# The last chunk's output stage laid out by two batches and 64 tokens, half of it run inside that chunk, and the second half of the preparation convolved by taps alone

## The reference

```python
x = x + _L0_cond_ref(x, ..., cond_2048, 16)          # attention, 16 heads
x = x + _L1_cond_ref(x, cond_2048, W_in, W_conv, ...)

def _L1_cond_ref(x, t_emb, W_in, W_conv, b_conv, ln_g, ln_b, W_xproj, W_dt, b_dt, A_log, D, W_out):
    xr, gate = jnp.split(x @ W_in.T, 2, axis=-1)     # 1024 channels each
    xr = xr + t_emb[:, None, :]
    xc = silu(causal_conv_of_4_taps(xr, W_conv) + b_conv)
    xn = layernorm(xc) * ln_g + ln_b
    Bm, Cm, dt = jnp.split(xn @ W_xproj.T, 3, axis=-1)   # 16 states each
    dt = jnp.tanh(dt @ W_dt.T + b_dt) * 0.01
    Ad = 1.0 + dt * A
    Bd = Bm * jnp.minimum(jnp.linalg.norm(xn, axis=-1, keepdims=True), 1.0)
    def step(h, inputs):                             # 1024 steps, one after the other
        ad, bd, xt, ct = inputs
        h = jnp.clip(h * ad[:, :, None] + bd[:, :, None] * xt[:, None, :], -10.0, 10.0)
        return (h, jnp.einsum('bd,bdh->bh', ct, h))
    _, ys = jax.lax.scan(step, h0, ...)
    y = ys + D * xn
    return y * jax.nn.silu(gate) @ W_out.T
```

## Time and profile before

| | us |
|---|---|
| median of three runs (6010.3 to 6031.31) | 6021.95 |
| profiled execution | 6045.26 |
| its span | 6043.3 |
| attention and the first half of the preparation | 0 to 3212.8 |
| second half of the preparation | 3212.8 to 3353.2 |
| recurrence, chunks 0 to 6 | 3353.2 to 5673.7 |
| recurrence, chunk 7 | 5673.7 to 5957.5 |
| tail | 5957.5 to 6043.3 |

### The profile page before, as it was taken

How to read it: one execution, slowest core, us unless ns; L and a number is a source line. 1 busy time by engine, 2 the same in 40 slices (tenths; PEclk the granted TensorE clock), 3 DMA queues, 4 the chain that set the end, 5 groups by cost and what they waited for, 6 DMA issues and landing times.

```text
span 6043.3 us, 74674 instructions
## 1 busy us (share of the span) xinstructions
PE 5770.7 (95%) x24986; PEld 2610.9 (43%) x24986; DVE 4388.4 (73%) x5652; ACT 2411.4 (40%) x4726; POOL 3185.9 (53%) x2561
## 2 busy tenths in 40 slices
PE   7999999999999999999989999999999999999999
PEld 3444444444444444444435434434344444434334
DVE  4656556565565656656534899999999999999994
ACT  2444444444444444444445333434243433434110
POOL 1777667776676767666664142434434242434313
PEclk7999999999999999999999999999999999999999
DMA  2332323323233232322322444444445344444543
GB/s 88 84 99 64 100 60 112 96 66 102 60 109 95 63 102 62 114 82 58 99 70 105 107 123 107 125 133 122 137 113 151 99 143 110 133 126 124 140 116 122
DMA packets 415984, 622.82 MB, mean 103 GB/s; under 512 B 59088, under 2 KB 192336, under 8 KB 415088
## 3 DMA queue, kind: packets, MB, share of 16 engines
q1 hardware_dynamic: 378736, 567.68, 33.2%
q10 hardware_dynamic: 36864, 50.38, 3.3%
HBM read 310.56 MB, written 205.57 MB: 85 GB/s over the span
## 4 chain that ended last, share of the span: by engine, by line
PE 70%; DVE 18%; issue 4%; ACT 2%; ACTq 2%; POOL 2%; DMA 1%; DVEq 1%; SPq 0%; POOLq 0%
DVE g L2223 9%; PE bank L820 8%; PE bank L850 8%; PE bank L808 6%; PE miscb L1979 5%; PE misc L837 5%; PE yps L1940 5%; DVE g L2229 5%; PE bank L779 3%; PE bank L761 3%; PE miscb L1871 3%; PE bank L789 3%; PE yps L1871 3%; PE xps L1926 2%; PE miscb L1950 2%
## 5 line engine op out<-in xcount | busy, mean ns | idle before, releaser
L1161 POOL TENSOR_TENSOR acc<-acc,prob 128x512 f32<-128x512 f32 x1536 | 1908.1, 1279 | 853.9 <-PE bank L850 571.7
L1090 DVE TENSOR_REDUCE mx<-bank 128x1 f32<-128x512 f32 x2048 | 1308.2, 686 | 542.7 <-PE bank L820 536.5
L2223 DVE SCALAR_TENSOR_TENSOR g<-xps,bd,g 128x1024 f32<-128x1024 f32 x1024 | 1313.1, 1282 | 118.9 <-PE xps L1926 89.6
L983 ACT ACTIVATE prob<-misc 128x512 f32<-128x512 f32 x1277 | 713.5, 598 | 760.7 <-PE misc L837 675.1
L820 PE MATMUL bank<-khat,qhat 96*128 96x512 f32 x2048 | 940.5, 520 | 20.5 <-DVE xt_s L1067 15.3
L2229 DVE TENSOR_SCALAR g<-g,lim 128x1024 f32<-128x1024 f32 x1024 | 832.1, 813 | 34.6
L837 PE MATMUL misc<-qhat,khat 98*128 98x512 f32 x1443 | 602.6, 460 | 18.2 <-ACT prob L983 12.4
L820 PEld LDWEIGHTS bank<-khat,qhat 96*128 96x128 f32 x2048 | 374.0, 192 | 548.7 <-issue 383.1
L1940 PE MATMUL yps<-g,cexp 128*32 128x512 f32 x4096 | 499.8, 606 | 0.0
L808 PE MATMUL bank<-xhT,wqk 128*128 128x512 f32 x1024 | 490.2, 605 | 2.6 <-ACT rsum L989 1.7
L850 PE MATMUL bank<-prob,V 128*32 128x512 f32 x3584 | 488.9, 615 | 0.2 <-ACT prob L983 0.2
(11 more groups left out here) (246 smaller groups left out, 7752.3 us busy)
## 6 DMA issues: line engine op xcount, KB each, us to landing
sx<-scratch_xhl SPq DMA_DIRECT2D x512, 128.0 KB, 5.3
scratch_dx<-dx SPq DMA_DIRECT2D x64, 512.0 KB, 2.8
scratch_xhl<-xhi SPq DMA_DIRECT2D x64, 512.0 KB, 4.0
scratch_xhl<-xn SPq DMA_DIRECT2D x64, 512.0 KB, 4.7
scratch_y<-ysb SPq DMA_DIRECT2D x512, 64.0 KB
early<-scratch_dx SPq DMA_DIRECT2D x59, 512.0 KB, 4.7
early<-scratch_y SPq DMA_DIRECT2D x59, 512.0 KB, 3.6
xt_n<-in_x SPq DMA_DIRECT2D x112, 256.0 KB, 3.0
```

Of the source, the lines that this page charges most:

```text
L983: act.activation(to, bank[m][:, 0:QC], ACT.Exp, scale=SCALE).then_inc(sem[f"act_m{m}"], 1)
L1090: dve.tensor_reduce(self.mx2[:, h * TT + qt, c:c + 1], bank[m][:, 0:QC], AX.X, ALU.max).then_inc(sem[f"dve_m{m}"], 1)
L1161: pool.tensor_tensor(self.acc[:, a, h, :], self.acc[:, a, h, :], self.prob[:, (n % 2) * GH + h, :], ALU.add).then_inc(sem["pool_acc"], 1)
L2223: dve.scalar_tensor_tensor(self.g[:, t % STATES, :], self.xps[t % 2][:, :], self.bd[:, i % 2, tl:tl + 1], self.g[:, (t - 1) % STATES, :], ...
```

## The change

The change has four parts.

- **Preparation.** `by_matmul` no longer names the channel tiles 1, 3, 5 and 7 of chunk 0's second half. They are convolved by taps.
- **Output stage of chunk 7.** A tile is now two batches and 64 tokens (`last_rows`): tiles 0 to 3 hold the first 64 tokens of all eight batches, tiles 4 to 7 the last 64. Tiles 0 to 3 run in room 1 inside chunk 7, due from 0.55 to 0.97 of it. Tiles 4 to 7 are the tail, in rooms 0 (4 and 7), 1 (5) and 2 (6). Each load and store of such a tile is two DMAs of 64 partitions instead of one of 128. The gates are loaded back between 0.02 and 0.5 of the chunk.
- **Planner's numbers.** `PE_LATE` goes from 0.3 to 0.2. In the preparation, fillers come only for gaps over 0.9 and in banks 3, 1 and 0. The ends of the lanes move a little.
- Chunk 6's output stage is due 0.1 of a chunk before the end of chunk 7, so that it doesn't meet the end.

```diff
-PE_LATE = 0.3
+PE_LATE = 0.2
-LAST_ROOMS = 3
+LAST_ROOMS = (4, 7), (0, 1, 2, 3, 5), (6,)
+def last_rows(b, TOK):
+    h, pair = divmod(b, 4)
+    return [(slice(64 * k, 64 * k + 64), 2 * pair + k, slice(h * TOK // 2, (h + 1) * TOK // 2)) for k in range(2)]
 def by_matmul(i, hb, ct):
-    return ct in ((2,5) if i == 1 else (1, 3, 5, 7) if (i, hb) == (0, 1) else ())
+    return ct in ((2,5) if i == 1 else ())
...
-    order.warm = (0.6, 0.15, 0.45, (3, 1, 0, 2))
+    order.warm = (0.9, 0.3, 0.45, (3, 1, 0))
...
+    order.warm = (0.6, 0.15, 0.45, (3, 1, 0, 2))
     order.lane(steps())
     for i in range(NCH):
         t = i * TOK
-        order.lane(expand(i, range(1, TOK // WIDE)), t - 4.0, t + 0.8 * TOK)
+        order.lane(expand(i, range(1, TOK // WIDE)), t - 4.0, t + 0.7 * TOK)
         if i + 1 < NCH:
-            order.lane(convolve(i + 1, SIDE), t + -8.0, t + 0.627 * TOK)
-            order.lane(rows(i + 1, SIDE), t + 0.143 * TOK, t + 0.937 * TOK)
+            order.lane(convolve(i + 1, SIDE), t + -8.0, t + 0.637 * TOK)
+            order.lane(rows(i + 1, SIDE), t + 0.144 * TOK, t + 0.937 * TOK)
         if i:
-            order.lane(finish(i - 1, SIDE, 0, range(B)), t + -8.0, t + TOK + (0.0 if i < NCH - 1 else -3.0))
+            order.lane(finish(i - 1, SIDE, 0, range(B)), t + -8.0, t + TOK + (0.0 if i < NCH - 1 else -0.1 * TOK))
...
         if i == NCH - 1:
-            order.lane(back(), t + 0.1 * TOK, t + 0.9 * TOK)
+            order.lane(back(), t + 0.02 * TOK, t + 0.5 * TOK)
+            order.lane(finish(i, SIDE, 1, range(4)), t + 0.55 * TOK, t + 0.97 * TOK)
     order.run(lambda: ("g", last - 1) in order.done)
     order.late = None
-    for room in range(LAST_ROOMS):
-        order.lane(finish(NCH - 1, ALL, room, range(room, B, LAST_ROOMS)), last - 1.0, last - 1.0)
+    for room, some in enumerate(LAST_ROOMS):
+        order.lane(finish(NCH - 1, ALL, room, [b for b in some if b >= 4]), last - 1.0, last - 1.0)
...
-                sp.dma_start(self.room[rm]["y"][:, :], d["y"][b, i * TOK:(i + 1) * TOK, :]).then_inc(sem[f"ld_y{rm}"], 16)
+                for rows, c, some in self.rows_of(i, b):
+                    sp.dma_start(self.room[rm]["y"][rows], d["y"][c, some, :]).then_inc(sem[f"ld_y{rm}"], 16)
```

63 lines of the change are left out of this document (39 added, 24 removed).

## The result

The changed kernel takes 5984.94 us (median of six runs, 5981.13 to 5998.19) and the kernel before 6021.61 us (six runs beside it, 6010.3 to 6031.31). The ratio is 0.9943, with an interval from 0.9928 to 0.9958: 36.7 us less, where 43 were forecast. The profiled execution took 5998.19 us with a span of 5996.4, 47 us less than the profiled one of before.

The account below looks back on a forecast made before the run. No engine was full in the preparation's second half; DVE bounds the recurrence and PE the tail. Tail 30, preparation 11, chunks between 9, less 7 in chunk 7, make 43 us: 6022 to 5979 us, with 5953 to 6004 holding 8 in 10.

Parts of the forecast that it names:

- The sum: Whole kernel: 30 + 11 + 9 - 7 = 43 us less, 6022 to 5979 us.
- The tail: After the last `g`: four of eight PE tiles go, 31.0 us less 1.0 us of small costs, 30 us gained.
- the preparation: Second half of the preparation: taps replace matmuls and `nrm` comes earlier, 11 us gained, bounds 4 and 17 us.
- the chunks between: Chunks 1 to 6: shorter waits for `x` through the limit of 0.2, 1.5 us a chunk, 9 us gained.
- chunk 7: Last chunk: four more `oo` on DVE cost 2.7 us and added waits for `x` 4.3 us, 7 us lost.
- three small things: Tail: second DMA of the first `y` tile 0.3 to 0.4 us, last tile's `om` wait 0.25, split last store 0.35.
- I am wrong if the tail isn't under 60 us: Sign for the tail: from the last `g` to the end 56 us was expected instead of 85.8.
- Rival 2: Chunk 7: PE's list stops for late `fs` or loads, two 2.1 us waits per tile, 17 us lost, 5995 us; chance 0.11.
- nrm comes at 3279 to 3280 instead of 3290.28: Preparation: after earlier transposes, store, statistics and root, `nrm` on ACT comes earlier, the basis of the 11 us gain.
- From there POOL is full for 40 us as before: Preparation, from `nrm` on: POOL works 40 us without a break and the end of the preparation is unchanged.
- rival 1: Preparation: twelve taps cost POOL's first half 9 us, the preparation gains only 2 us, 5988 us; chance 0.13.
- Rival 4: Seven chunks: PE's clock falls once more in each, DVE waits 4.9 us, 34 us lost, 6013 us; chance 0.07.

Follow-up runs that it names:

- a_fill: The changed kernel with more fillers in the tail (54 behind the last outputs instead of 39): 5979.72 us, tail 62.6 us.
- b_split: The kernel before, last chunk's output-stage loads and stores as two DMAs of 64 neighbouring partitions each: 6034.54 us, tail 90.3 us.
- b_even: The kernel before, last chunk's output-stage loads and stores as two DMAs, one of even and one of odd partitions: 6020.47 us, tail 88.4 us.
- a_first: The changed kernel with the last lanes due 3.5 steps later, so SP stores the last outputs before loading `D * xn`: 5983.63 us, tail 64.4 us.
- b_wolate: The kernel before with the load of `w_out` put off to the first chunk: 6018.27 us, preparation 134.8 us.
- a_matmul: The changed kernel with the preparation's four channel tiles convolved by matmul again: 5988.07 us, preparation 138.1 us.
- b_late2: The kernel before with `PE_LATE` at 0.2 instead of 0.3 and nothing else: 6019.73 us, chunks 0 to 6 2318.6 us.
- b_lanes: The kernel before with only the changed kernel's three due times of the loop's lanes: 6027.17 us, chunks 1 to 6 1982.8 us.
- a_loopfill: The changed kernel with more fillers on PE in the loop (idle gap 0.4 us instead of 0.6): 5987.03 us.
- a_one: The changed kernel with one DMA per load and store, two batches by 64 tokens in one pattern, instead of two: 6125.22 us.

## Why the prediction was right, point by point

**The sum.** -43 forecast, -36.7 by the medians and -40.0 by the stages that the change touches. The sign and the stages are those forecast; the terms are not. The tail gave 8.6 us less than forecast and the preparation 2.6 less; the chunks between gave 4.5 more and chunk 7 cost 3.7 less. That the sum comes within 3 us is in part luck.

**The tail, the mis-sized term.** "The tail gives 31.0 - 1.0 = 30 us": it gave 21.4. The four tiles did go at the price forecast. In a_fill, with its fillers, the tail behind the first `yt` takes 36.2 us, and the forecast's 56 us less the 19.9 up to it are 36.1. The mistake is in the "three small things" that come back. I priced two DMAs of 64 partitions by the time to issue the second, 0.3 to 0.4 us, and took their rate for granted. The traces show 5.9 us up to the first transpose; in the three other traces with the order of the changed kernel's tail it is 4.9 to 5.7, and their tails take 63.0 to 63.6 us. b_split has the part that the split alone costs, 2.6 us, and b_even shows that 2.2 of it are the rate of neighbouring partitions. The other 3.3 us are argued and not isolated by a run. The loads of `D * xn` stood 3.7 us ahead of the last `g` in the kernel before and now stand behind a store of chunk 7, 0.8 us ahead: 1.5 MB meet the last outputs on their way. a_first shows that this can't be had back by moving the store. That the two halves of a load now come from two batches is a rival that no run separates from it. Last, PE ran out of fillers over the longer wait, and its clock cost 2.3 us (a_fill). 5.9 + 2.3 = 8.2 of the 8.6 us that the term is short. "I am wrong if the tail isn't under 60 us": this step was wrong.

**Chunk 7.** +3.3 us, where 2.7 + 4.3 were forecast. Four `oo` more of 0.68 us are 2.7 us by their durations, and DVE's busy time rose by 2.1. The waits rose from 2.2 to 3.1 us, and not by 4. The denser end of the chunk costs almost nothing, since the order puts the tiles between the `x`. Rival 2 is refuted by the longest wait of 1.1 us.

**The preparation.** -8.4 us for -11, but by another way. The step "nrm comes at 3279 to 3280 instead of 3290.28" fell short. The stage begins 6.8 us earlier in the trace of the change, so it has to be read from the stage's start: forecast were 10 to 11 us less, and `nrm` starts 69.8 us after it where it started after 77.5, 7.7 less. It was lost at the taps. They were to end near 3260.5, 47.7 us after the start, and end after 53.9: DVE is busy with the last twenty-one for 27.3 us, within the 31 of the forecast, but it stops for 6.0 us among them, 3.4 of that for one scaling on ACT. `hi` and `sq` stand behind the last silu on ACT's list, and the first half's last `lo` ends after 61.6 us, with 57.8 forecast and 67.6 before. "From there POOL is full for 40 us as before" failed: it took 45.8 us, with stops of 3.99 and 0.89 us for ACT and 1.54 for a store, since ACT now has the attention's evictions among its copies. I moved `f_mm` of tiles 2 to 4 behind the projections on PE and didn't follow their evictions on ACT's list. These are -7.7 and +6.4 us; the other -7.1 came behind the last `lo`. What made up for the lost time stood in brackets as a bound: the load of `w_out`. That it came out near the forecast is luck. b_wolate gives 5.7 us by it alone, and of the 6 us that a_matmul loses, 5.3 lie between the last `lo` and the first `q`, behind that load. As to what taps and POOL cost each other: POOL's pairs of passes beside the taps took 2.94 to 3.41 us instead of 2.50, which makes 5.4 us over the first half and 1.8 in the kernel before. The twelve more taps cost POOL 3.6 us, 0.30 us each, between the 0.15 of the rows and the 0.75 that the rule of the Trainium skill (SBUF — State Buffer, Who interferes with whom) comes to if taken strictly. It cost the kernel nothing, since each group of slowed passes ends in a stop of POOL for ACT (5.41, 1.30 and 0.34 us); rival 1 priced the loss at 9 us and fell. DVE paid more: its eighteen taps beside POOL took 1.39 us on average, where one alone takes 0.78, and ACT's work stood behind them.

**The chunks between.** -13.5 us for chunks 0 to 6 where -9 was forecast, and the cause given was wrong. `PE_LATE` alone gives nothing (b_late2). The lanes' due times do it (b_lanes), +3.0 us in chunk 0 and 3.4 us off each of chunks 2 to 5. The forecast took the stretches at the lower clock as given and shortened the short waits; it gave 0.5 us to what had moved in such a stretch. The traces show the reverse: the time at the lower level falls from 13.7 to 6.8 us a chunk in chunks 2 to 5, and the 3.4 us go with it. Rival 4, that the clock falls once more in each chunk, didn't come; the opposite did. Its price of 4.9 us was a fair one: chunk 5 of a_loopfill, where it did fall, took 4.8 us more than its neighbour.

## What to carry to other kernels

Before a tile is laid differently over the partitions, read the rate of the DMAs that fill it in the last two columns of a window: a half-tile of 64 neighbouring partitions moved at 0.6 of the rate with the engines just as busy, and a pattern with an outer dimension of two ran at the share of two engines of sixteen. Where a stage ends in a short load that everything waits for, look at what else was sent for in the 20 us before; a 2 MB load there cost 6 us, and moving it is one line. When work leaves one engine's list, follow the results of that work on the next engine's list, since that is where part of the gain went here. And before a few microseconds in a loop are put down to an edit, compare the same chunk in traces of the same order, and the time that each spent at the lower clock: here that alone made 3.3 us of 331.

## What the runs showed that was not expected

- The rate by partitions: 383 GB/s for DMAs of 128 partitions, 234 and 237 for 64 neighbouring ones, 279 at a share of 0.84 for 64 alternate ones. Laying the changed kernel's two batches on even and odd partitions would join the two; it wasn't tried.
- One DMA over [2, 64] rows: share 0.13, 53 GB/s.
- An issue can cost far more than the 0.33 to 0.6 us that most take here: four DMAs of 256 KB took 7.97 us to issue with 2 MB ahead of them, 4.04 us without, and in a_one a single one took SP 12 us (6042.26).
- In chunks 1 to 6 a microsecond of PE at its lower clock goes with about half a microsecond more, though DVE and not PE is the limit there.
- Between executions the attention part, over 3190 us, moved by 23 us with no change in it, which is more than half of the effect that was measured.
